# A share of the weight splitting in a mixture of experts moves to GpSimd

## The reference

```python
rn = layernorm(x) * ln_gamma + ln_beta                 # 512 tokens, 512 features
rw, sel = top_k(softmax(rn @ gate_w.T), 2)             # two experts for each token
h = gelu(einsum('nc,efc->enf', layernorm_x, w1))       # w1: 8 x 1024 x 512, float32
y = einsum('enf,ecf->enc', h, w2)                      # w2: 8 x 512 x 1024, float32
out = x + sum over the two chosen experts of rw * y
```

## Time and profile before

| | |
|---|---|
| median of 3 runs | 934.28 us (933.08 to 936.36) |
| the profiled execution, device time | 938.36 us |
| its span in the trace | 936.6 us |
| busy: PE, DVE, ACT, POOL | 879.1, 677.9, 527.7, 387.2 us |
| POOL busy of that: additions of L472 | 247.4 us |
| mixture's tiles | about 750 to 936 us of the span |

### The profile page before, as it was taken

One profiled execution on the slowest core, in us unless ns is written; L12 is line 12 of the kernel. 1 busy time (PEld: TensorE's weight loads), 2 busy tenths in 40 slices (PEclk: granted clock), 3 DMA queues, 4 the chain that ended last, 5 costly groups with the idle time before them and its releaser, 6 DMA issues. The chain is left out here.

```text
span 936.6 us, 24792 instructions
## 1 busy us (share of the span) xinstructions
PE 879.1 (94%) x10509; PEld 625.3 (67%) x10509; DVE 677.9 (72%) x1022; ACT 527.7 (56%) x811; POOL 387.2 (41%) x294
## 2 busy tenths in 40 slices
PE   5999999999999999999999999989888899998995
PEld 2565777776676776776867867755546787766663
DVE  7856787656688655688656556667778678989993
ACT  3644445565354564354565554552657278989893
POOL 1131775445576445566445555536230042111122
PEclk9999999999999999999999999999989999999999
DMA  9364122442121441221342211308414739999982
GB/s 341 119 170 117 27 68 60 135 125 76 41 70 39 121 134 37 60 57 47 82 125 80 70 38 33 93 2 304 171 54 164 284 126 361 406 401 401 400 280 34
DMA packets 48456, 134.69 MB, mean 144 GB/s; under 512 B 9894, under 2 KB 11814, under 8 KB 44494
## 3 DMA queue, kind: packets, MB, share of 16 engines
q1 hardware_dynamic: 45354, 126.81, 40.2%
q0 software_dynamic: 2800, 6.04, 3.2%
q10 hardware_dynamic: 192, 0.26, 0.1%
HBM read 95.03 MB, written 11.31 MB: 114 GB/s over the span
## 5 line engine op out<-in xcount | busy, mean ns | idle before, releaser
L472 POOL TENSOR_TENSOR acc_pool<-acc_pool,pT 128x1024 f32<-128x1024 f32 x90 | 212.0, 2356 | 146.3 <-ACT pT L742 144.7
L742 ACT ACTIVATE pT<-ps_s 128x1024 f32<-128x1024 f32 x124 | 126.9, 1023 | 196.5 <-PE ps_s L928 196.5
L578 DVE TENSOR_REDUCE mpart<-ps_b 128x1 f32<-128x512 f32 x256 | 173.4, 684 | 72.1 <-PE ps_b L908 71.3
L892 PE MATMUL ps_a<-wv_hi,cT_hi 128*128 128x128 f16 x1024 | 183.5, 219 | 0.0
L894 PE MATMUL ps_a<-wv_hi,cT_lo 128*128 128x128 f16 x1024 | 182.7, 219 | 0.0
L893 PE MATMUL ps_a<-wv_lo,cT_hi 128*128 128x128 f16 x1024 | 182.6, 219 | 0.0
L573 DVE TENSOR_TENSOR k_lo<-k_f,k_hi 128x512 f16<-128x512 f32 x64 | 76.4, 1194 | 58.1 <-ACT k_hi L715 58.1
L892 PEld LDWEIGHTS ps_a<-wv_hi,cT_hi 128*128 128x128 f16 x1024 | 99.8, 97 | 7.9 <-issue 6.0
L893 PEld LDWEIGHTS ps_a<-wv_lo,cT_hi 128*128 128x128 f16 x1024 | 100.2, 98 | 7.2
L894 PEld LDWEIGHTS ps_a<-wv_hi,cT_lo 128*128 128x128 f16 x1024 | 99.8, 97 | 0.0
L908 PE MATMUL ps_b<-k_stack,q_stack 101*128 101x512 f16 x256 | 96.8, 381 | 2.3 <-DMA k_stack<-k_lo 1.3
(11 more groups left out here) (290 smaller groups left out, 1855.5 us busy)
## 6 DMA issues: line engine op xcount, KB each, us to landing
w_raw<-in_w SPq DMA_DIRECT2D x30, 2048.0 KB, 17.0
raw<-in_context SPq DMA_DIRECT2D x16, 1024.0 KB, 6.2
k_stack<-k_hi SPq DMA_DIRECT2D x252, 64.0 KB, 2.0
k_stack<-k_lo SPq DMA_DIRECT2D x128, 64.0 KB, 2.0
slots_in<-a_zeros SPq DMA_DIRECT2D x1, 3855.0 KB, 13.7
rows_in<-slots_in SPq DMA_DIRECT2D x15, 257.0 KB, 17.2
q_stack<-k_stack SPq DMA_DIRECT2D x12, 128.0 KB, 2.4
x_sb<-in_x SPq DMA_DIRECT2D x2, 512.0 KB, 4.1
```

Source lines behind the costliest of these rows:

```text
L472: nc.gpsimd.tensor_tensor(acc_pool[:, :], pT[:, 0, :] if p == 1 else acc_pool[:, :], pT[:, p % PT, :], ALU.add).then_inc(pool_add, 1)
L578: nc.vector.tensor_reduce(mpart[:, j, kb:kb + 1], bank_at(step)[:, :], AX.X, ALU.max).then_inc(p1_max, 1)
L742: nc.scalar.activation(pT[:, p % PT, :], scores(w, p)[:, :], ACT.Exp, scale=SM_SCALE).then_inc(exp_done, 1)
L892: nc.tensor.matmul(to, cT_hi[:, c, keys], t.wv_hi[:, c, col], start=(c == 0), stop=False)
```

## The change

The last two of the eight row blocks of w2 (`POOL_BLOCKS`), 1024 elements per partition, are split by GpSimd for tiles 1 to 14: three instructions, a multiplication by 64 in place, a copy to float16 (hi) and a subtraction (lo), each counted in a new semaphore `w2_pool` and each waiting for the one before. ScalarE and VectorE still work in two parts, now of three blocks, 1536 elements, each. GpSimd does the share of tile k + 2 ahead of the scatter of tile k. Down waits for `w2_pool` too, and so does the load of w2 two tiles later on SyncE. To have a semaphore for it, the two of the bias functions become one, with counts to match.

```diff
@@ cross attention
-        bias_mm, row_out, bias_out = sem("bias_mm"), sem("row_out"), sem("bias_out")
+        bias_mm, bias_out = sem("bias_mm"), sem("bias_out")
...
-                nc.scalar.activation(bias_row[n], bias_bank(n)[0][0:1, :], ACT.Copy).then_inc(row_out, 1)
+                nc.scalar.activation(bias_row[n], bias_bank(n)[0][0:1, :], ACT.Copy).then_inc(bias_out, 1)
...
-                act.wait_ge(bias_out, n + 1)
+                act.wait_ge(bias_out, 2 * n + 2)
...
-                pe.wait_ge(row_out, n + 1)
-                if n:
-                    pe.wait_ge(bias_out, n)
+                pe.wait_ge(bias_out, 2 * n + 1)
...
@@ mixture
+POOL_BLOCKS = 2
...
         def w2_split(w, i):
-            return w[:, NF // 2 * i:NF // 2 * (i + 1), :]
+            n = (NF - POOL_BLOCKS) // PARTS
+            return w[:, n * i:n * (i + 1), :]
+
+        def w2_pool_part(w):
+            return w[:, NF - POOL_BLOCKS:NF, :]
+
+        def w2_pool_parts(k):
+
+            return 3 * k
...
             def w2_load(k):
                 sp.wait_ge(w2_lo_s, w2_parts(k - 2))
+                sp.wait_ge(w2_pool, w2_pool_parts(k - 2))
...
+            def w2_share(k):
+
+                u = k % 2
+                pool.wait_ge(w2_in[u], 16 * uses(k))
+                if k >= 2:
+                    pool.wait_ge(down, k - 1)
+                raw, hi, lo = [w2_pool_part(w[u]) for w in (w2_raw, w2_hi, w2_lo)]
+                nc.gpsimd.tensor_scalar(raw, raw, W_SCALE, None, ALU.mult).then_inc(w2_pool, 1)
+                pool.wait_ge(w2_pool, w2_pool_parts(k) - 2)
+                nc.gpsimd.tensor_copy(hi, raw).then_inc(w2_pool, 1)
+                pool.wait_ge(w2_pool, w2_pool_parts(k) - 1)
+                nc.gpsimd.tensor_tensor(lo, raw, hi, ALU.subtract).then_inc(w2_pool, 1)
+
             pool.wait_ge(s.out_sem, 16 * (NB + 1))
+            w2_share(1)
             for k in range(TILES):
+                if k + 2 < TILES:
+                    w2_share(k + 2)
                 pool.wait_ge(y_out, k + 1)
...
             def down_tile(k):
                 pe.wait_ge(h_lo_s, 2 * (k + 1))
                 pe.wait_ge(w2_lo_s, w2_parts(k))
+                if k:
+                    pe.wait_ge(w2_pool, w2_pool_parts(k))
```

More of the change, by code:

```diff
@@ L789, in bias_in_a_row @@
                 if n == 1:
-                    pe.wait_ge(row_out, n)
+                    pe.wait_ge(bias_out, 2 * n - 1)
                 if n == 2:
@@ L871, in _ @@
                             pe.wait_ge(w_lo, 3)
-                            pe.wait_ge(bias_out, 2)
+                            pe.wait_ge(bias_out, 4)
                     bank, col, keys = bank_at(step[:3]), slice(P * g, P * (g + 1)), slice(KB * kb, KB * (kb + 1))
@@ L1553, in mixture @@
                                                  sem("m_y_out"))
-        y_added, copied = sem("y_added"), sem("m_copied")
+        y_added, copied, w2_pool = sem("y_added"), sem("m_copied"), sem("m_w2_pool")
         def w1_split(w, i):
```

## The result

The changed kernel takes 953.91 us (953.58 to 958.45, 4 runs) where the kernel before takes 935.32 (933.08 to 942.24, 4 runs; the three of before and one more): a ratio of 1.0197, with a 95% interval of 1.0135 to 1.026. So it is slower, by 1.4 to 2.6%. The profiled execution took 953.58 us with a span of 951.6.

What follows compares the result with a forecast made beforehand. It took the weight transfers to bound the mixture, VectorE having 1.02 us spare per tile, and VectorE to bound it after. 934.28 plus 21.8 (50.7 - 15.0 - 13.9) gave 956 us, 8-in-10 range 934 to 984.

Steps and rivals of the forecast that it cites:

- What goes: Mixture: VectorE's w2 instruction shrinks from 2048 to 1536 elements, saving 1.07 us per tile, 15.0 us over 14 tiles.
- The collision: Mixture: VectorE's two-SBUF-input instructions wait for GpSimd's three, losing 3.9 us per tile, 50.7 us over 13 shares.
- What is taken up: Mixture: VectorE's waits for ScalarE go when VectorE is late itself, giving back 13.9 us.
- The sum: VectorE's w2 stretch over tiles 1 to 14: 50.7 - 15.0 - 13.9 = +21.8 us.
- The signs: Mixture: w2 instruction far above 1.75 us, w1 instruction above 2.28, x_low still 0.68, DMA share below 1.00.
- they take turns, each for a whole instruction: Mixture: GpSimd's SBUF-reading instructions and VectorE's two-SBUF-input ones exclude each other throughout; GpSimd's share priced at 4.96 us per tile.
- The waits added: New waits on SP's loads, POOL's scatters and TensorE's down: no cost beyond the sum; scatters up to 7 us later.
- the share itself comes last: Rival: GpSimd's share ends 0.3 us behind the 7.0 down leaves, thirteen times, without delaying VectorE: 938 us, chance 0.07.
- the share fits the gaps: Rival: only the subtraction delays VectorE, 2.1 us per tile, transfers still set 11.7: 931.3 to 932.8 us, chance 0.19.

Runs made afterwards that it cites:

- the kernels with memsets: Changed kernel with GpSimd's three instructions replaced by six write-only memsets: 940.91 us with the share ahead of the scatter, 938.19 us with it behind.
- the third experiment: Changed kernel with GpSimd making only hi of the last two blocks, by one multiplication per tile, VectorE subtracting all eight blocks: 939.77 us, 1.0032 of before.
- the kernel with four blocks: Changed kernel with GpSimd's share doubled to four of eight row blocks, three instructions of 2048 elements per tile: 1017.25 us, 1.0875 of before.

## Why the prediction was right

The forecast was 956 and the mechanism is the one forecast: VectorE bounds the mixture, since it stands while GpSimd reads. That the sum came so close is in part luck, as said below under the sizes. By steps, in the profiled executions:

- *What goes.* 28 instructions of 1.74 instead of 2.29 us: 15.3 us saved, predicted 15.0.
- *The collision.* Against their undisturbed busy time, the lines of VectorE grew by 16.7, 7.7 and 24.0 us, 48.4 in all, predicted 50.7:

```profile
L1804 DVE SCALAR_TENSOR_TENSOR cT_lo<-w_raw,cT_hi 128x2048 f16<-128x2048 f32 x26 | 75.0, 2923 | 0.3 <-ACT cT_hi L1837 0.3
L1811 DVE SCALAR_TENSOR_TENSOR parts<-w_raw,parts 128x1536 f16<-128x1536 f32 x28 | 55.7, 2027 | 0.3 <-ACT parts L1845 0.3
L1820 DVE SCALAR_TENSOR_TENSOR h_lo<-h_f,h_hi 128x512 f16<-128x512 f32 x29 | 43.1, 1518 | 4.8 <-ACT h_hi L1900 4.8
L1666 POOL TENSOR_SCALAR w_raw<-w_raw 128x1024 f32<-128x1024 f32 x14 | 51.3, 3664 | 12.3 <-DMA w_raw<-in_w 12.3
L1668 POOL CAST parts<-w_raw 128x1024 f16<-128x1024 f32 x14 | 29.3, 2092 | 0.9
L1670 POOL TENSOR_TENSOR parts<-w_raw,parts 128x1024 f16<-128x1024 f32 x14 | 48.2, 3443 | 1.2
```

- *What is taken up.* VectorE's waits for ScalarE fell by 15.8, predicted 13.9.
- *The sum.* 48.4 - 15.3 - 15.8 = +17.3, where +21.8 was predicted. In the timeline VectorE's stretch from the first w2 pair to the end of the last grew from 155.5 to 173.0 us (765.07 to 938.03), +17.5. The medians differ by 18.6, the spans by 15.0, since the stretch began 2.9 us earlier in this execution; the w1 pair ahead of it, before any share, already stood 2.5 us earlier.
- *The signs.* L1811 has a mean of 2.03 us and L1804 of 2.92, and x_low keeps 0.68, as was said. The transfers' share fell only from 1.00 to 0.97, so that sign was a weak one; their rate says more, 361 GB/s for 386.
- *Where sizes were off.* The copy (1.24 alone) and the subtraction (2.45) were priced well at 1.3 and 2.36, the multiplication badly: 2.8 us at the least, not 1.3. And "they take turns, each for a whole instruction" fits the additions of the earlier trace rows and, nearly, the copy and the subtraction, but not the multiplication, which holds VectorE for only 0.83 of its 2.8 us. The two errors cancel, and that is luck: with whole turns and the right lengths the share would be 6.5 us, the loss 5.4 per tile, and the same sum would have given +42, 976 us. GpSimd's busy time rose by 129 us, not 70, as its instructions stand in their turns too: the means above are 3.7, 2.1 and 3.4 us.
- *The waits added.* SP's loads and the scatters cost nothing while VectorE leads, as was said: from 765 to 930 us VectorE waits for nothing. At the end, the last scatter at 945.51 waited for the one before, 1.3 us after y was there at 944.20, for 0.8 us before, so 0.5 us are the scatters'. Without the collision the same waits are worth some 4 us. The rival "the share itself comes last" (938) was close in number to the 940.9 and 938.2 of the kernels with memsets, but not in its account: it has TensorE late in thirteen tiles and the last scatter waiting for y, where in the first of the two that scatter waits for the one before and y is not late.
- *The rival "the share fits the gaps"* falls: VectorE loses 3.6 us per tile, and up to 2.1 would have fitted. Nor did the one instruction of the third experiment fit, with no work taken off VectorE: there the last y came 4.0 us later in the stretch.

## What to carry to other kernels

In this kernel work given to GpSimd was paid for by VectorE wherever GpSimd read SBUF while VectorE read two SBUF inputs. Before moving elementwise work there, add to VectorE's work what it loses to each of GpSimd's reading instructions and compare the sum with the period, instead of looking at each engine's idle share: here 9.6 + 3.6 = 13.2 us for a period of 11.7. Their lengths are not that loss: at 2.8, 1.24 and 2.45 us, 6.5 in all, VectorE lost 0.84, 0.83 and 1.93. Run one such instruction beside the busy engine and read the loss. Such collisions can be read from the kernel before, if the two engines meet anywhere in it: look for instructions of one line whose longest is a multiple of the shortest, and for ends at a fixed distance behind GpSimd's. And where a transfer sets the period, shortening the engines beside it buys little: with VectorE's work 1.07 us shorter per tile and no reads by GpSimd, the stretch to the last y stayed at 161.7 us. Only a shorter end gained something here, 0.2%.

## What the runs showed of the hardware that was not expected

- A multiplication by a constant on GpSimd, 128x1024 float32 to float16, lasts 2.77 us alone, a copy of that size 1.24. The Trainium skill, "GPSIMD Engine Reference", section "Engine selection", calls one-input work roughly line rate, by which my estimate was 0.85; the measured numbers decide. What VectorE lost to either of them, 0.83 to 0.84 us, is near that estimate; their length is not.
- That multiplication holds a VectorE instruction for 0.84 us, or for 1.9 in six tiles of the third experiment in which it starts before the scatter ahead of it has ended. That is not the whole condition: in the changed kernel it also starts so, at 847.12 beside a scatter that ends at 847.18, and the w2 pair loses 0.84. Why is open.
- In the kernel with four blocks TensorE's granted clock was 0.88 on the mean, so in part at the lower of its two levels, with TensorE busy for 97 of 130 us (windows as in the earlier trace rows) and standing up to 4.1 us ahead of an up; it had been 1.00 with 124 of 130:

```profile
775.00:905.00 130.00, 97.27 (x892) 69.72 (x892) 130.00 (x52) 67.95 (x74) 127.75 (x30) 0.88 0.77 280
```
